# The last batch's group norm moved one step forward into other PSUM banks, and one clearing moved behind the first mixed input, in a two-layer kernel

## The chip, the cores and the metric

The kernel runs on one core of a Trainium2 chip. The metric is the device time of one execution in microseconds (us). The kernel before was run three times: median 1484.47 us, lowest 1482.65, highest 1484.83. One more execution was taken with the hardware profiler; its rows are used below.

## The reference, cut to what matters

16 batches of 112 tokens by 512 channels go through two layers. The first is a cross attention over 375 context rows. The second is an RWKV block, and only this one is touched. For each batch:

```python
xa = ln(x); sx = shift(xa) - xa
xxx = tanh((xa + sx * maa_x) @ maa_w1)          # the "mixed input" xa + sx * maa_x
xk, xw, xv, xr, xg = xa + sx * (maa_stack + xxx @ maa_w2)
w = exp(-exp(time_decay + tanh(xw @ td_w1) @ td_w2))
r, k, v, g = xr @ Wr.T, xk @ Wk.T, xv @ Wv.T, silu(xg @ Wg.T)
# scan over the tokens, state per head: out = r (u k v + s);  s = k v + w s
m, va = mean(out), var(out)                     # per head: the group norm
og = (out - m) / sqrt(va + 1e-5) * gn_w + gn_b
x1 = x + og * g @ Wo.T
xc = ln(x1); xk2, xr2 = xc + sx2 * ffn_maa_k, xc + sx2 * ffn_maa_r
return x1 + sigmoid(xr2 @ Wfr.T) * (square(relu(xk2 @ Wfk.T)) @ Wfv.T)
```

## The kernel before

All five engines run instruction streams written out by hand, ordered by semaphores. The first phase (`cross_attention`) does the first layer for all batches and writes each result to DRAM. Then `rwkv_block`, the second phase, begins with a barrier.

The second phase is a pipeline of 18 steps over 16 batches, three batches deep. `step(n)` does `pre` for batch n (layer norm, mixing, the projections r, k, v, g), `scan` for batch m = n - 1 (the recurrence over chunks of 8 tokens), and `post` for batch l = n - 2 (group norm, output projection, second layer norm, feed-forward part). A batch is one tile: channels on 128 partitions, 4 groups of channels times 112 tokens = 448 elements in the free direction. Each engine has its own `step` function, which writes down the order of these parts on that engine. TensorE's is unrolled over all 18 steps; the other engines loop over pairs of steps.

Steps at the ends are thin. Step 0 has `pre` only. Step 16 has `scan` of batch 15 (the last) and `post` of batch 14. Step 17 has `post` of batch 15 alone.

The PSUM banks are dealt out by role. `pre_bank` (three banks, b_bank3 to b_bank5) serves the layer norm's transposes, the mixing and the projections. `post_bank` (b_bank6 and b_bank7) serves everything in `post`. So batch l's mean (`gn_mean`, L1660, into `post_bank[0]`) waits until the batch before it has read its feed-forward result out of that bank (`s_ff`, incremented by `finish`, L1178).

The chain of the last batch, with its lines: `wkv_sum` on DVE (L1128), `gn_mean` on PE (L1660), `centre` on DVE (L1136), `square` on ACT (L1401), `gn_var` on PE (L1667), `gn_rstd` on ACT (Ln L1407, Exp L1409, each behind a table load), `group_norm` on DVE (L1141), `gn_affine` on ACT (L1268), `gate_output` on POOL (L926), `project_out` on PE (L1504 with b_wo), `residual` and second layer norm on DVE (L1146 to L1155), transposes on PE (L1491), `xc_affine` on ACT, `ffn_input` on DVE (L1167), `ffn_key` (L1498 with b_wfk), `ffn_receptance` (b_wfr) and `ffn_value` (b_wfv) on PE, `finish` on DVE (L1178, L1181) and the store. The centred values live in `cen` and their squares and inverse deviations in `sq`; `cen` is also the input xr2 of `ffn_receptance`.

The start of the second phase, with its lines: statistics of batch 0 on DVE, `rstd1` (L882) and `xa_state` (L887) on POOL, `apply1` on DVE (L1010), transposes on PE, `xa_affine` on ACT, `token_shift` (L1018) and `mix_input` (L1023) on DVE. Behind `mix_input`, DVE runs `setup` (L984 to L990: seven small tensor_scalar operations on constants). PE then does `maa_first` (L1522, L1524) and `maa_second` (L1552); DVE does `mix` (L1034), POOL adds (`mix`, L899), PE goes on with `decay_first` (L1562). On POOL, `zero_blocks` (L873 to L878) stands directly behind `xa_state`: five memsets of the buffers wz, kz, vbd and first. Their values are first needed by ACT's `decay_factor` near the end of step 0.

Of the kernel before, what the change touches and what calls it, by code (L numbers as in the profile page):

```python
# [678 lines left out]
def rwkv_block(nc, A, ident, vec, W, w_loaded, K, k_loaded):  # L679
# [3 lines left out]
    with ExitStack() as ctx:  # L683
# [94 lines left out]

        def by_chunk(flat):

            return flat.rearrange("p (c b s) -> p c b s", c=C, s=CH)
# [82 lines left out]
        def _(pool):  # L864
# [54 lines left out]
            def gate_output(l, scan):  # L919
                pool.wait_ge(s_gaff, count(l, 1, 1))  # L920
                pool.wait_ge(s_g, count(l, 1, 1))
                if at_least(l, 1):
                    pool.wait_ge(s_wo, count(later(l, -1), 1, 1))
                if scan:
                    pool.wait_ge(s_bonus, count(later(l, 1), 1, 1))
                pool.tensor_tensor(gated[:], sq[:], gate2[:, l[1]], ALU.mult).then_inc(s_gated, 1)  # L926
# [54 lines left out]
        def _(dve):  # L981
# [149 lines left out]
            def centre(l):  # L1131
                dve.wait_ge(s_mean, count(l, 1, 1))
                if at_least(l, 1):
                    dve.wait_ge(s_gaff, count(later(l, -1), 1, 1))
                    dve.wait_ge(s_fr, count(later(l, -1), 1, 1))
                dve.tensor_tensor(cen[:].rearrange("p c t -> p (c t)"), wkv[:].rearrange("p c t -> p (c t)"),  # L1136
                                  post_bank[0][:, 0:CT], ALU.subtract).then_inc(s_cen, 1)

            def group_norm(l):
                dve.wait_ge(s_grs, count(l, 1, 1))  # L1140
                dve.tensor_tensor(cen[:], cen[:], sq[:], ALU.mult).then_inc(s_gnorm, 1)  # L1141
# [42 lines left out]
            def step(n, pre, scans, post, first):  # L1184
# [13 lines left out]
                if post:  # L1198
                    wkv_sum(l)
# [17 lines left out]
                if post:  # L1217
                    centre(l)
# [4 lines left out]
                if post:  # L1223
                    group_norm(l)
# [38 lines left out]
        def _(act):  # L1263
# [133 lines left out]
            def square(l):  # L1397
                act.wait_ge(s_cen, count(l, 1, 1))
                if at_least(l, 1):
                    act.wait_ge(s_gated, count(later(l, -1), 1, 1))  # L1400
                act.activation(sq[:], cen[:], ACT.Square).then_inc(s_sq, 1)  # L1401

            def gn_rstd(l):

                act.wait_ge(s_var, count(l, 1, 1))
                flat = sq[:].rearrange("p c t -> p (c t)")
                act.activation(flat, post_bank[1][:, 0:CT], ACT.Ln, bias=ln_eps[:, 0:1]).then_inc(s_ln2, 1)  # L1407
                act.wait_ge(s_ln2, count(l, 1, 1))
                act.activation(flat, flat, ACT.Exp, scale=-0.5).then_inc(s_grs, 1)  # L1409

            def gn_affine(l):
                act.wait_ge(s_gnorm, count(l, 1, 1))
                affine(lambda c: sq[:, c], lambda c: cen[:, c], half_gn[:, 0], half_gn[:, 1]).then_inc(s_gaff, 1)
# [23 lines left out]
            def step(n, pre, scans, post, first):  # L1437
# [18 lines left out]
                if post:  # L1456
                    square(l)
                if pre:
                    decay_rate(n)
                if post:  # L1460
                    gn_rstd(l)
                    gn_affine(l)
# [12 lines left out]
                if post:  # L1475
                    relu_square(l)
                    receptance(l)

# [3 lines left out]
        def _(pe):  # L1482
# [173 lines left out]
            def gn_mean(l):  # L1656
                pe.wait_ge(s_wkv, count(l, 1, 1))
                if at_least(l, 1):
                    pe.wait_ge(s_ff, count(later(l, -1), 1, 1))
                pe.matmul(post_bank[0][:, 0:CT], headmean[:], wkv[:].rearrange("p c t -> p (c t)"), start=True,  # L1660
                          stop=True).then_inc(s_mean, 1)

            def gn_var(l, scans):
                pe.wait_ge(s_sq, count(l, 1, 1))
                if scans:
                    pe.wait_ge(s_bv, count(later(l, 1), 1, 1))
                pe.matmul(post_bank[1][:, 0:CT], headmean[:], sq[:].rearrange("p c t -> p (c t)"), start=True,  # L1667
                          stop=True).then_inc(s_var, 1)

            def project_out(l):  # L1670
                pe.wait_ge(s_gated, count(l, 1, 1))
                token_major(post_bank[0], weight(l, "wo"), gated).then_inc(s_wo, 1)
# [5 lines left out]
            def ffn_key(l):  # L1678
                pe.wait_ge(s_xk2, count(l, 1, 1))
                channel_major(post_bank[0], weight(l, "wfk"), xk2).then_inc(s_fk, 1)  # L1680
# [9 lines left out]
            def step(n, pre, scans, post, first):  # L1690
# [15 lines left out]
                if post:  # L1706
# [6 lines left out]
                if post:  # L1713
                    gn_var(l, scans)
# [121 lines left out]
```

## Time and profile before

| what | value |
|---|---|
| median of 3 runs | 1484.47 us (1482.65 to 1484.83) |
| the profiled execution's own time | 1483.6 us |
| its span (first to last instruction) | 1481.8 us |
| mean granted TensorE clock over the span | 0.973 |
| busy share PE / DVE / ACT / POOL | 94% / 60% / 49% / 33% |
| second phase | from about 653 us to the end |

Times in the trace are counted from the start of the span. "Busy" of an engine leaves out waits. A row of the timeline gives start, duration, engine, line, operation, the tiles written and read, and in square brackets the idle time of the engine before it and who ended it. In the names, `b_bank` stands for any of the eight banks, `xk` for xk2, `rk` is also `gated`, `x` for x2, `ln_tok` also for ln2_tok, which `receptance` writes. One matmul instruction in float32 shows as two MATMUL records (x8 is four instructions).

### The profile page before, as it was taken

What the parts mean: (1) busy time and instruction counts of PE and PEld (TensorE: products, weight loads), DVE (VectorE), ACT (ScalarE), POOL (GpSimd) and SP (SyncE); (2) the same over time, 40 slices, a digit from 0 to 9 for tenths busy, and PEclk for the clock granted to TensorE, in tenths of its full rate; (3) what the DMA queues carried; (4) which work ended last, traced back from release to release, by engine and by line L of the source; (5) the groups of instructions that cost most, each with busy time, mean ns of one, the idle gap of its engine ahead of it and who ended that gap; (6) DMA issues with size and microseconds to landing.
All of it is one profiled execution on the core that took longest, in us unless ns stands there. A gap on an engine that the chain in (4) does not pass through costs nothing. (4 is left out here: it accounts for less than half of the span.)

```text
span 1481.8 us, 41201 instructions
## 1 busy us (share of the span) xinstructions
PE 1388.5 (94%) x16448; PEld 1007.6 (68%) x16448; DVE 888.9 (60%) x2287; ACT 722.5 (49%) x1772; POOL 486.7 (33%) x530
## 2 busy tenths in 40 slices
PE   5999999999999999947989999999999999999965
PEld 4777777777777777626766667666676666666632
DVE  3444444444444443433887788887878878787751
ACT  3666666666666666521245344443444434444422
POOL 2211111111111111011543456434554345543330
PEclk9999999999999999968899999999999999999997
DMA  7531111111111100012001000011000010010000
GB/s 217 152 92 41 41 41 40 39 39 39 39 38 35 34 24 14 7 32 105 11 20 27 27 20 9 25 26 26 19 10 26 26 27 8 20 26 21 20 13 6
DMA packets 25686, 54.97 MB, mean 37 GB/s; under 512 B 3984, under 2 KB 6672, under 8 KB 24016
## 3 DMA queue, kind: packets, MB, share of 16 engines
q1 hardware_dynamic: 25552, 52.99, 12.4%
q8 instruction: 108, 1.77, 0.5%
q14 instruction: 26, 0.21, 0.0%
HBM read 42.23 MB, written 7.34 MB: 33 GB/s over the span
## 5 line engine op out<-in xcount | busy, mean ns | idle before, releaser
L907 POOL TENSOR_TENSOR rst<-rp,st 128x448 f32<-128x448 f32 x192 | 193.9, 1029 | 74.4 <-DVE st L1105 49.7
L270 POOL TENSOR_TENSOR aT_lo<-whole,aT_hi 128x375 fp32r<-128x375 f32 x64 | 58.6, 916 | 443.9 <-ACT whole L422 441.1
L342 DVE CUSTOM_DVE_ANT_0 probs<-a_bank,unmask 112x375 f32<-112x375 f32 x256 | 126.0, 545 | 79.7 <-PE a_bank L539 72.4
L899 POOL TENSOR_TENSOR xm<-mixed,xa 128x448 f32<-128x448 f32 x80 | 87.8, 1097 | 240.6 <-DVE mixed L1034 239.1
L441 ACT ACTIVATE probs<-probs,least 112x375 f32<-112x375 f32 x256 | 153.8, 607 | 0.0
L348 DVE RECIPROCAL inv_rows<-sums 112x128 f32<-112x128 f32 x64 | 61.0, 953 | 153.9 <-ACT probs L441 153.9
L450 ACT COPY probsT<-a_bank 125x448 f32<-125x448 f32 x192 | 90.1, 535 | 51.7 <-PE a_bank L594 51.7
L1034 DVE SCALAR_TENSOR_TENSOR mixed<-b_bank,vec_sb,sx 128x112 f32<-128x112 f32 x320 | 83.1, 328 | 53.5 <-PE b_bank L1552 52.7
L594 PEld LDWEIGHTS a_bank<-ident_sb,probs 112*125 112x125 f32 x768 | 90.8, 188 | 30.9 <-ACT keyT L432 16.3
L594 PE MATMUL a_bank<-ident_sb,probs 112*125 112x112 f32 x768 | 99.3, 279 | 2.7 <-ACT probs L441 2.7
L537 PE MATMUL a_bank<-aT_hi,wk_lo 128*128 128x376 f32 x256 | 91.1, 356 | 1.7 <-issue 1.7
L539 PE MATMUL a_bank<-aT_hi,wk_hi 128*128 128x376 f32 x256 | 85.3, 333 | 0.0
L538 PE MATMUL a_bank<-aT_lo,wk_hi 128*128 128x376 f32 x256 | 84.8, 331 | 0.0
L537 PE MATMUL a_bank<-wv_hi,aT_lo 128*126 128x512 f32 x192 | 79.9, 416 | 0.0
L1268 ACT ACTIVATE xa<-b_bank,vec_sb 128x112 f32<-128x112 f32 x64 | 23.2, 444 | 110.0 <-POOL xm L899 88.9
L538 PE MATMUL a_bank<-wv_lo,aT_hi 128*126 128x512 f32 x192 | 75.7, 394 | 0.0
L539 PE MATMUL a_bank<-wv_hi,aT_hi 128*126 128x512 f32 x192 | 75.6, 394 | 0.0
L1113 DVE TENSOR_TENSOR rst<-rp,st 128x448 f32<-128x448 f32 x64 | 74.9, 1171 | 0.7 <-PE b_bank L1609 0.7
L1084 DVE TENSOR_TENSOR bv<-bv,ktil 128x392 f32<-128x392 f32 (+6 forms) x112 | 69.5, 621 | 3.8
L436 ACT COPY value<-a_bank 125x512 f32<-125x512 f32 x48 | 28.1, 586 | 85.6 <-PE a_bank L539 85.6
L1504 PE MATMUL b_bank<-b_wo,rk 128*112 128x512 f32 x128 | 61.8, 629 | 7.2 <-POOL rk L926 7.2
L1609 PE MATMUL b_bank<-rst,b_collect 128*32 128x448 f32 x512 | 58.3, 548 | 6.3 <-DVE rst L1113 5.3
(167 smaller groups left out, 3100.0 us busy)
## 6 DMA issues: line engine op xcount, KB each, us to landing
ctx_tok<-in_ctx SPq DMA_DIRECT2D x16, 750.0 KB
xT_sb<-in_xT SPq DMA_DIRECT2D x16, 224.0 KB, 9.7
x_tok<-in_x SPq DMA_DIRECT2D x16, 224.0 KB, 9.4
x_between_layers<-x_sb SPq DMA_DIRECT2D x16, 224.0 KB, 2.3
b_x<-x_between_layers SPq DMA_DIRECT2D x16, 224.0 KB, 2.7
x_post<-x_between_layers SPq DMA_DIRECT2D x16, 224.0 KB, 2.8
out_dram<-fin SPq DMA_DIRECT2D x16, 224.0 KB, 2.3
vbd<-vtok SPq DMA_DIRECT2D x208, 16.0 KB
```

What stands on the lines that cost most here:

```text
L342: dve.tensor_tensor_reduce(out=probs[:, g % 2, i], in0=score_bank[i][0:T, 0:TC], in1=unmask[:, m[1]], scale=-SCALE, scalar=-LOWEST, op0=AL ...
L441: act.activation(probs[:, g % 2, i], probs[:, g % 2, i], ACT.Exp, scale=-1.0, bias=least[:, g % 2, i:i + 1], accum_out=sums[:, g % 2, i:i ...
L450: act.copy(probsT[:, g % 2, k], unit_bank(n, f"P{g}{k}")[0:TK, 0:HG * T]).then_inc(s_ringev, 1)
L537: pe.matmul(dst, ll, rh, start=start, stop=False)
L538: pe.matmul(dst, lh, rl, start=False, stop=False)
L539: return pe.matmul(dst, lh, rh, start=False, stop=stop)
L594: last = pe.transpose(dst[0:TK, i * T:(i + 1) * T], probs[:, g % 2, i, k * TK:(k + 1) * TK], ident[0:T, 0:T])
L899: pool.tensor_tensor(xm[:, f % 2], mixed[:, f % 2], xa[:, :, 1:T + 1], ALU.add).then_inc(s_xm, 1)
L907: pool.tensor_tensor(by_chunk(rst[:, j % NPROD]), by_chunk(rp[:].rearrange("p c t -> p (c t)")), state_of(j), ALU.mult).then_inc(s_pprod, 1)
L1034: last = dve.scalar_tensor_tensor(out=mixed[:, f % 2, c], in0=src[:, c * T:(c + 1) * T], scalar=vec[:, VEC[MIXES[f]], c:c + 1], in1=sx[:, ...
L1084: dve.tensor_tensor(dst, dst, vprod[:, :, 0:CH - d], ALU.add).then_inc(s_acc, 1)
L1113: dve.tensor_tensor(by_chunk(rst[:, j % NPROD]), by_chunk(rp[:].rearrange("p c t -> p (c t)")), state_of(j), ALU.mult).then_inc(s_vprod, 1)
```

## The change

It does two things.

1. On POOL, `zero_blocks` waits for the first mixed input of batch 0 (`s_xin`, incremented by the last instruction of `mix_input`) before its first memset.

2. For the last batch alone (`is_last`), `wkv_sum`, `gn_mean`, `centre`, `square`, `gn_var`, `gn_rstd`, `group_norm` and `gn_affine` are issued in step 16 instead of step 17. The mean goes to `pre_bank[0]`, the variance to `pre_bank[1]`, the output projection to `pre_bank[2]`; the centred values and squares live in `xm[:, 0]` and `xm[:, 1]`, since the last batch's projections have read these by then. New waits stand for the new owners of these buffers: `s_mixed`, `s_r`, `s_g`, `s_gmm`, and `s_fin` and `s_ff` of the batch in front where `post_bank[0]` and x2 are used again.

```diff
+        def is_last(l):
+            return is_batch(l, B - 1)
+        def norm_home(l):
+            return (xm[:, 0], xm[:, 1]) if is_last(l) else (cen[:], sq[:])
+        def norm_bank(l):
+            return (pre_bank[0], pre_bank[1]) if is_last(l) else (post_bank[0], post_bank[1])
+        def out_home(l):
+            return pre_bank[2] if is_last(l) else post_bank[0]
...
             def zero_blocks():
+                pool.wait_ge(s_xin, 1)
                 pool.memset(wz[:], 0.0)
...
             def centre(l):
                 dve.wait_ge(s_mean, count(l, 1, 1))
-                if at_least(l, 1):
+                if is_last(l):
+                    dve.wait_ge(s_gmm, count(l, 1, 1))
+                elif at_least(l, 1):
...
             def residual(l):
                 dve.wait_ge(s_wo, count(l, 1, 1))
                 dve.wait_ge(s_x1p[l[1]], 16 * (l[0] + 1))
+                if is_last(l):
+                    dve.wait_ge(s_fin, count(later(l, -1), 1, 1))
-                dve.tensor_tensor(x2[:], post_bank[0][0:T, :], x1p[:], ALU.add).then_inc(s_x2, 1)
+                dve.tensor_tensor(x2[:], out_home(l)[0:T, :], x1p[:], ALU.add).then_inc(s_x2, 1)
...
# VectorE's step (and "if post and not is_last(l)" where these three stood)
                 if post:
                     ffn_input(l, xk2, "ffn_k", s_xk2)
+                    if is_last(m):
+                        wkv_sum(m)
                     ffn_input(l, xr2, "ffn_r", s_xr2)
+                if is_last(m):
+                    centre(m)
+                    group_norm(m)
...
# ScalarE's step
                 if post:
                     relu_square(l)
+                if is_last(m):
+                    square(m)
+                if post:
                     receptance(l)
+                if is_last(m):
+                    gn_rstd(m)
+                    gn_affine(m)
...
             def gn_mean(l):
                 pe.wait_ge(s_wkv, count(l, 1, 1))
-                if at_least(l, 1):
+                if is_last(l):
+                    pe.wait_ge(s_mixed, count(l, MAA, MAA))
+                elif at_least(l, 1):
                     pe.wait_ge(s_ff, count(later(l, -1), 1, 1))
...
# TensorE's step
                 if post:
                     ffn_key(l)
+                if is_last(m):
+                    gn_mean(m)
+                if post:
                     ffn_receptance(l)
+                if is_last(m):
+                    gn_var(m)
```

Nothing is added to or taken from the work; no DMA is moved. The order of instructions is shown at three places, with the line numbers of each kernel's own file (the change shifts them). The first is PE at the end of the program, the kernel before: the last rows of step 16, then step 17 (from the second L1660 on).

```order
L1498 MATMUL b_bank6<-xk2,b_wfk 64x112 x32
L1504 MATMUL b_bank7<-b_wfr,cen 112x512 x4
L1504 MATMUL b_bank6<-b_wfv,xk2 112x512 x4
L1660 MATMUL b_bank6<-wkv,b_headmean 128x448
L1667 MATMUL b_bank7<-sq,b_headmean 128x448
L1504 MATMUL b_bank6<-b_wo,rk 112x512 x4
L1491 MATMUL b_bank7<-ident_sb,ln2_tok 128x112 x4
```

The same stretch of PE in the changed kernel.

```order
L1531 MATMUL b_bank6<-xk2,b_wfk 64x112 x32
L1695 MATMUL b_bank3<-wkv,b_headmean 128x448
L1537 MATMUL b_bank7<-b_wfr,cen 112x512 x4
L1704 MATMUL b_bank4<-xm,b_headmean 128x448
L1537 MATMUL b_bank6<-b_wfv,xk2 112x512 x4
L1537 MATMUL b_bank5<-b_wo,rk 112x512 x4
L1524 MATMUL b_bank7<-ident_sb,ln2_tok 128x112 x4
```

The mean and the variance of batch 15 now stand on either side of batch 14's receptance, ahead of batch 14's ffn_value, in banks 3 and 4.

The second is ACT at the same place, before: relu and square of batch 14's key, its tanh, then batch 15's square, logarithm and exponential.

```order
L1427 ACTIVATE xk2<-b_bank6 128x448
L1429 ACTIVATE xk2<-xk2 128x448
L1435 ACTIVATE ln2_tok<-b_bank7 112x512
L1401 ACTIVATE sq<-cen 128x448
L1407 ACT_TABLE_LOAD
L1407 ACTIVATE sq<-b_bank7,b_eps 128x448
L1409 ACT_TABLE_LOAD
```

And in the changed kernel.

```order
L1454 ACTIVATE xk2<-b_bank6 128x448
L1456 ACTIVATE xk2<-xk2 128x448
L1428 ACTIVATE xm<-xm 128x448
L1462 ACTIVATE ln2_tok<-b_bank7 112x512
L1434 ACT_TABLE_LOAD
L1434 ACTIVATE xm<-b_bank4,b_eps 128x448
L1436 ACT_TABLE_LOAD
```

Batch 15's square moved ahead of batch 14's tanh; the two table loads stand directly behind the tanh.

The third is POOL at the start of the second phase in the changed kernel.

```order
L890 MEMSET wz 128x1080 [waits xin_ready]
L891 MEMSET kz 104x1024
L892 MEMSET vbd 104x4096
L893 MEMSET chunk_first 128x540
L895 MEMSET chunk_first 128x4x14 [waits first_cleared]
```

The order of the rows is that of before (there L873 to L878); only the wait for xin_ready is new.

## Rows read from the trace of the kernel before

**Rows 1.** The page: its first line.

```profile
span 1481.8 us, 41201 instructions
```

**Rows 2.** Windows: stretch, length, busy per engine, granted clock, DMA share, GB/s.

```profile
650.00:698.00 48.00, 25.74 (x396) 23.08 (x396) 18.32 (x48) 6.56 (x22) 13.25 (x18) 0.75 0.27 103
767.03:1325.44 558.41, 556.54 (x8118) 381.46 (x8116) 451.89 (x1046) 243.29 (x565) 270.18 (x276) 1.00 0.08 21
```

**Rows 3.** Timeline of the second phase's start, up to the first transposes.

```profile
657.23 0.19 POOL L887 COPY xa<-b_rows 128x4 f32<-128x4 f32 x1
657.31 6.15 DVE L1010 TENSOR_SCALAR ln_tok<-b_x,ln_mv,ln_rs 112x512 f32<-112x512 f32 x1 [0.78 <-POOL ln_rs L882]
657.36 1.00 POOL L873 MEMSET wz<- 128x1080 f32 x1
...
663.25 0.36 POOL L878 MEMSET chunk_first<- 128x56 f32 x1
```

**Rows 4.** Line L1010 alone: min/median/max ns over its 16 instructions.

```profile
L1010 DVE TENSOR_SCALAR ln_tok<-b_x,ln_mv,ln_rs x16: 535/544/6154, 657.3 to 1325.4; 112x512 f32<-112x512 f32 x16
```

**Rows 5.** Timeline, from the mixed input to the first decay product.

```profile
666.78 1.07 DVE L1023 SCALAR_TENSOR_TENSOR xin<-sx,vec_sb,xa 128x112 f32<-128x112 f32 x4
...
668.04 0.87 DVE L990 TENSOR_SCALAR bonus_w<-b_same_head,vec_sb 128x128 f32<-128x128 f32 x4
...
673.03 1.06 DVE L1034 SCALAR_TENSOR_TENSOR mixed<-b_bank,vec_sb,sx 128x112 f32<-128x112 f32 x4 [4.12 <-PE b_bank L1552]
...
674.15 1.43 PE L1552 MATMUL b_bank<-th,b_maa 32*64 32x112 f32 x16 [1.14 <-DVE mixed L1034]
674.17 1.05 POOL L899 TENSOR_TENSOR xm<-mixed,xa 128x448 f32<-128x448 f32 x1 [10.57 <-DVE mixed L1034]
...
675.50 1.75 PE L1562 MATMUL b_bank<-xm,b_td 128*64 128x112 f32 x8
```

**Rows 6.** Timeline: VectorE beside GpSimd's unbroken run, and GpSimd beside VectorE's.

```profile
720.88 3.75 POOL L907 TENSOR_TENSOR rst<-rp,st 128x448 f32<-128x448 f32 x4
720.95 4.04 DVE L1084 TENSOR_TENSOR bv<-bv,ktil 128x336 f32<-128x336 f32 x1
...
783.92 2.30 POOL L917 TENSOR_TENSOR rk<-rec,key 128x448 f32<-128x448 f32 x1 [2.67 <-ACT rec L1333]
...
784.15 1.06 DVE L1023 SCALAR_TENSOR_TENSOR xin<-sx,vec_sb,xa 128x112 f32<-128x112 f32 x4
```

**Rows 7.** Timeline of the program's end, to the output projection of batch 15.

```profile
1433.75 3.69 PE L1504 MATMUL b_bank<-b_wfr,cen 128*112 128x512 f32 x8
...
1434.45 0.58 ACT L1429 ACTIVATE xk<-xk 128x448 f32<-128x448 f32 x1
...
1437.48 0.60 ACT L1435 ACTIVATE ln_tok<-b_bank 112x512 f32<-112x512 f32 x1 [2.45 <-PE b_bank L1504]
...
1441.74 0.99 PE L1660 MATMUL b_bank<-wkv,b_headmean 128*128 128x448 f32 x2 [0.87 <-DVE fin L1178]
...
1442.77 0.62 DVE L1136 TENSOR_TENSOR cen<-wkv,b_bank 128x448 f32<-128x448 f32 x1 [0.45 <-PE b_bank L1660]
...
1444.02 1.28 ACT L1407 ACT_TABLE_LOAD   x1
...
1451.38 6.06 PE L1504 MATMUL b_bank<-b_wo,rk 128*112 128x512 f32 x8 [6.30 <-POOL rk L926]
```

**Rows 8.** TensorE's timeline, a full step: what follows the mean's matmul.

```profile
895.94 1.02 PE L1660 MATMUL b_bank<-wkv,b_headmean 128*128 128x448 f32 x2
896.89 0.99 PE L1569 MATMUL b_bank<-ttd,b_td 128*64 128x112 f32 x16
```

**Rows 9.** Windows over projections out (batch 14, batch 15) and key (batch 15).

```profile
1414.81:1420.19 5.38, 5.38 (x8) 1.87 (x8) 1.20 (x3) 0.00 (x0) 4.87 (x5) 0.68 0.00 2
1451.38:1457.44 6.06, 6.06 (x8) 2.17 (x8) 0.00 (x0) 0.00 (x0) 0.00 (x0) 0.60 0.00 0
1464.89:1470.57 5.68, 5.68 (x65) 5.54 (x65) 0.93 (x4) 0.00 (x0) 0.00 (x0) 0.56 0.00 0
```

More of the change, by code:

```diff
@@ L1197, in step @@
                         decay_key(m, d)
-                if post:
+                if post and not is_last(l):
                     wkv_sum(l)
@@ L1216, in step @@
                     mix(n, 2)
-                if post:
+                if post and not is_last(l):
                     centre(l)
@@ L1222, in step @@
                     product(m, 3)
-                if post:
+                if post and not is_last(l):
                     group_norm(l)
@@ L1398, in square @@
                 act.wait_ge(s_cen, count(l, 1, 1))
-                if at_least(l, 1):
+                if at_least(l, 1) and not is_last(l):
                     act.wait_ge(s_gated, count(later(l, -1), 1, 1))
-                act.activation(sq[:], cen[:], ACT.Square).then_inc(s_sq, 1)
+                act.activation(norm_home(l)[1], norm_home(l)[0], ACT.Square).then_inc(s_sq, 1)
             def gn_rstd(l):
                 act.wait_ge(s_var, count(l, 1, 1))
-                flat = sq[:].rearrange("p c t -> p (c t)")
-                act.activation(flat, post_bank[1][:, 0:CT], ACT.Ln, bias=ln_eps[:, 0:1]).then_inc(s_ln2, 1)
+                flat = norm_home(l)[1].rearrange("p c t -> p (c t)")
+                act.activation(flat, norm_bank(l)[1][:, 0:CT], ACT.Ln, bias=ln_eps[:, 0:1]).then_inc(s_ln2, 1)
                 act.wait_ge(s_ln2, count(l, 1, 1))
@@ L1455, in step @@
                     tanh_td(n)
-                if post:
+                if post and not is_last(l):
                     square(l)
@@ L1459, in step @@
                     decay_rate(n)
-                if post:
+                if post and not is_last(l):
                     gn_rstd(l)
@@ L1657, in gn_mean, with gn_var @@
                 pe.wait_ge(s_wkv, count(l, 1, 1))
-                if at_least(l, 1):
+                if is_last(l):
+                    pe.wait_ge(s_mixed, count(l, MAA, MAA))
+                elif at_least(l, 1):
                     pe.wait_ge(s_ff, count(later(l, -1), 1, 1))
-                pe.matmul(post_bank[0][:, 0:CT], headmean[:], wkv[:].rearrange("p c t -> p (c t)"), start=True,
+                pe.matmul(norm_bank(l)[0][:, 0:CT], headmean[:], wkv[:].rearrange("p c t -> p (c t)"), start=True,
                           stop=True).then_inc(s_mean, 1)
-            def gn_var(l, scans):
+            def gn_var(l):
                 pe.wait_ge(s_sq, count(l, 1, 1))
-                if scans:
+                if is_last(l):
+                    pe.wait_ge(s_r, count(l, 1, 1))
+                else:
                     pe.wait_ge(s_bv, count(later(l, 1), 1, 1))
-                pe.matmul(post_bank[1][:, 0:CT], headmean[:], sq[:].rearrange("p c t -> p (c t)"), start=True,
+                pe.matmul(norm_bank(l)[1][:, 0:CT], headmean[:], norm_home(l)[1].rearrange("p c t -> p (c t)"), start=True,
                           stop=True).then_inc(s_var, 1)
@@ L1679, in ffn_key @@
                 pe.wait_ge(s_xk2, count(l, 1, 1))
+                if is_last(l):
+                    pe.wait_ge(s_ff, count(later(l, -1), 1, 1))
                 channel_major(post_bank[0], weight(l, "wfk"), xk2).then_inc(s_fk, 1)
@@ L1705, in step @@
                     decay_first(n)
-                if post:
+                if post and not is_last(l):
                     gn_mean(l)
@@ L1712, in step @@
                     attend_near(m, 1)
-                if post:
-                    gn_var(l, scans)
+                if post and not is_last(l):
+                    gn_var(l)
                 if pre:
```

15 lines of the change are left out of this document (9 added, 6 removed).

## The prediction

> **What bounds the kernel now.** I read the page first, for the span of 1481.8 us [rows 1], then the windows over the stages. In the twelve full steps of the second phase TensorE is busy for 556.5 of 558.4 us at full granted clock [rows 2]; the change leaves those steps alone, and nothing it does there could show. What is left are the ends. The first 48 us of the second phase have TensorE busy for 25.7 us, at a mean clock of 0.75 [rows 2], so there a chain through all engines sets the time; the same holds for the end, where one batch is alone. So the next view is the timeline of each end, read link by link: who starts when, and who was waited for.
>
> At the start the striking row is DVE's L1010, the normalisation of batch 0: 6.15 us [rows 3], where the median of its 16 runs is 0.544 [rows 4]. TensorE's first transposes wait for it. It began at 657.31, while POOL ran L887 (657.23 to 657.42), and ended at 663.46. POOL's clearing began at 657.36 and its last memset started at 663.25 [rows 3]. So the normalisation was held as long as POOL had one instruction ready behind the other, and was let go at the first pause. The same thing shows elsewhere: L1084, started 0.07 us behind a run of four products on POOL that ended at 724.63, ended at 724.99 [rows 6].
>
> At the end the chain of batch 15 begins with its mean, at 1441.74, and what it waited for is batch 14's finish on DVE, which frees the bank (the row's bracket names fin). From there the chain goes to the output projection at 1451.38, with TensorE idle for 6.30 us before it [rows 7].
>
> **The change, the start.** Without memsets behind L887, L1010 runs as its median: from 657.31, plus at most the 0.11 us that L887 still lasts, it ends near 657.86 instead of 663.46. That is **5.60 us** off the chain. In what follows I keep the times of before and speak of delays against them.
>
> The clearing itself now starts with the mixed input, whose last instruction ends at 667.85. What is next on each engine? On DVE the setup, seven small tensor_scalars without a pause, the last ending at 668.91 [rows 5]. They are of L1010's kind, so one of the two must wait. DVE is in the middle of its run when POOL wakes, and rows 6 show how that goes the other way round as well: POOL's L917, started at 783.92 while DVE ran without a pause, took 2.30 us and ended at 786.22, 1.01 after the end of DVE's mixed input (785.21), so it did next to nothing before. I take it that the clearing waits for the setup's end. It lasts from 657.36 to 663.61, 6.25 us [rows 3], so it runs from 668.91 to 675.16. Behind it on POOL stands the first add L899, which before began at 674.17 and took 1.05 [rows 5]: now it ends at 676.21. Who waits for it is decay_first (L1562), which began at 675.50, when TensorE was through with L1552 anyway. So 0.7 us are given back, and the chain behind (decay, the projection of v) moves by it. Bounds: 0 if setup and clearing pass each other (the clearing then ends by 674.3), 1.9 and more in the first rival. Net of the start: **-4.9 us**. The cleared buffers are asked for only at the end of step 0, so their being late costs nothing. DVE's own mix L1034, at 673.03, reads PSUM and one SBUF tile; I take it as undisturbed. The Trainium skill (SBUF — State Buffer, "Who interferes with whom") says that a VectorE instruction with at most one SBUF input outside the two-port modes does not contend with GpSimd; no row of this trace shows it beside a memset.
>
> **The change, the end.** Moving wkv_sum between the two inputs of batch 14's feed-forward part delays the second by about 0.6 us (the centring, an operation of the same shape, takes 0.62), hidden under ffn_key on TensorE, behind which the receptance began only at 1433.75 [rows 7]. Now gn_mean is issued there, at 1433.75. Its matmul holds TensorE for 0.95 us (895.94 to 896.89) [rows 8], so batch 14's receptance runs from 1434.70 and ACT's tanh, which ended at 1438.08, ends at 1439.03. The mean is there at 1434.74, the centring (0.62) at 1435.4, the square at 1436.0: ACT is free, since its last square of the key ends at 1435.03, and it waits for the receptance anyway. gn_var follows the receptance at 1438.1 and is through by 1439.2. So the chain now hangs on ACT: the table load of the logarithm follows the tanh, at 1439.04, where it came at 1444.02 [rows 7]; it ends after the variance is there. From that load to the output projection all links are as before (7.36 us). The projection starts **4.98 us** earlier.
>
> What is put back: batch 14's ffn_value ended at 1440.87 (the mean at 1441.74 less its idle 0.87) and now ends at 1442.8, two matmuls of 0.95 later, and its finish on DVE with it. The finish now stands behind group_norm of batch 15, which ends near 1443.5, and ahead of the residual, which waits for a projection that begins at 1446.4: hidden, with some 6 us to spare. The idle time of TensorE before the projection shrinks from 6.30 to 3.6 us. The projection of batch 15 took 6.06 us at a granted clock of 0.60, that of batch 14, with matmuls sparse before it but no long gap, 5.38 at 0.68 [rows 9]. At full clock eight such records take 3.69 (L1504, rows 7); at half clock throughout it would be about 7. I take 5.38, the row of the same instruction with less idle time before it: **0.68 us** more. The bounds are 2.4 gained and 0.9 lost. The key's 5.68 us at a clock of 0.56 [rows 9] can move by as much: half clock throughout would add 0.8, a clock that rises earlier would take off up to 2. I leave it.
>
> **The sum.** Start -4.9, end -4.98 - 0.68: -10.5 us. The profiled execution took 1483.6 us (span 1481.8), 0.9 below the median of the three runs; it becomes 1473.1, and the median of 1484.47 becomes **1474.0**, 0.7% less. A measurement of this kernel can tell about 0.2%, 3 us.
>
> **The rivals.**
>
> *The clearing holds the setup (0.20).* If POOL's memsets get in between two of DVE's small instructions, L990 waits for the run's end as L1010 did. The clearing then runs from 667.9 to 674.2, the setup ends at 674.9 instead of 668.91, the first mix starts at 674.9 instead of 673.03, and the transfer to decay_first is late by 1.9 instead of 0.7: 1475.2. For it speaks that L1010 lost against exactly this run; against it, that L917 had to wait for DVE's run.
>
> *They take turns (0.06).* Each waits for the other's one instruction. L1010 then should have come in after the first memset, at 658.4, and it did not [rows 3]; so little speaks for it. Five setup instructions beside the first four memsets (6.0 us) and about 1.2 us of their own: the setup ends near 675.2, 2.2 us late at the first mix: 1475.5. This is what the Trainium skill's page (SBUF — State Buffer, "SBUF: two separate sides") would give: the pair of ports goes to whoever starts first, for the whole instruction, and the other blocks. By that rule, taken for one instruction at a time, the time would be 1475.5. Rows 3 and 6 show a hold over a whole run of instructions instead.
>
> *The clearing is not what held L1010 (0.06).* Then something else at that moment did, the store or loads of x1 for example, and only the end gains, 5.7 us: 1478.8. Against it: L1010 ends within 0.3 us of the clearing's first pause.
>
> *The end does not gain (0.05).* The waits for other banks or an unlucky order on ACT eat it, for instance when the receptance's input comes late behind wkv_sum and the tanh with it; every microsecond that the tanh ends later than 1439.03 is lost in full. At 5 us it is all gone: 1479.6.
>
> *Slower (0.03).* The one mechanism that could turn the sign is TensorE's clock in the thin steps. The start ran at a mean clock of 0.75 [rows 2], falling and rising with the work, and the change shifts when the work comes. A busy microsecond's work at 2.4 GHz takes two at 1.2, so each further microsecond at the lower level costs up to 0.5. To eat 10.5 us, 21 further microseconds of busy TensorE would have to run at the lower level; from there on the kernel is slower. With 30 it would be 1474.0 + 15 = 1489.0. Against it: the twelve full steps ran at 1.00, the thin steps around them keep their order, and the gaps at both ends get shorter.
>
> **How the numbers follow.** The forecast has 0.60. The range takes in it and the two rivals of the lock: 1475.5 plus 1.7 us for a clock that stays low in the last projections and plus the spread of the runs, 1478.0 at the top; at the bottom 1474.0 less 0.7 (no collision), less 1.7 for a projection at full clock, less 1.3 for the key and the spread: 1470.3. That leaves out the other three rivals and little more. Faster by over 0.2% (below 1481.5) are all cases but the last: 0.95, with 0.03 for no change to be seen, where small losses add up to one of the weak rivals, and 0.02 for slower.
>
> **What would show it.** Start: L1010's counterpart lasts 0.5 to 0.7 us; the memsets start right behind the setup, and the first add on POOL behind them, about 2 us after the mix. If the last of the setup lasts 6 us, it is the first rival; if each is stretched a little, the second. End: the logarithm's table load directly behind batch 14's tanh, and the projection out 7.4 us behind that load. The twelve full steps keep their 46.5 us each (558.4 / 12). The forecast is wrong if L1010 stays long, if the projection starts less than 4 us closer to batch 14's receptance than before, or if the clock in either end differs by more than a tenth.

## The result, and the profile after

The changed kernel took 1474.41 us in the median of 11 runs (1472.26 to 1480.41), the kernel before, in 11 runs beside it, 1484.33 (1482.65 to 1485.79). The ratio is 0.9944 with a 95% interval of 0.993 to 0.9959: faster by 0.4 to 0.7%. Two more comparisons of the same kernel, told below, gave 0.9933 and 0.9952. The forecast was 1474.0 in a range of 1470.3 to 1478.0.

The profiled execution took 1472.61 us. Its page begins:

```profile
span 1470.8 us, 41203 instructions
...
PE 1388.6 (94%) x16448; PEld 1009.8 (69%) x16448; DVE 885.2 (60%) x2287; ACT 723.2 (49%) x1772; POOL 486.3 (33%) x530
```

The span is 11.0 us shorter than before [rows 1]. Of this, 1.1 us lies in the first phase, which the change does not touch: the second phase's first statistics on DVE start at 654.34, before at 655.43. From there to the start of the last instruction on DVE the changed kernel is 9.9 us shorter. All comparisons of profiles below are counted from that first statistics instruction for this reason.

The start of the second phase in the timeline of the changed kernel (its lines are higher than those of before: by 17 on DVE and POOL, by 27 on ACT, by 33 on PE):

```profile
656.15 0.19 POOL L904 COPY xa<-b_rows 128x4 f32<-128x4 f32 x1
656.23 0.55 DVE L1027 TENSOR_SCALAR ln_tok<-b_x,ln_mv,ln_rs 112x512 f32<-112x512 f32 x1 [0.78 <-POOL ln_rs L899]
656.83 1.01 PE L1524 MATMUL b_bank<-ident_sb,ln_tok 112*128 112x112 f32 x4 [8.54 <-DVE ln_tok L1027]
...
660.09 1.07 DVE L1040 SCALAR_TENSOR_TENSOR xin<-sx,vec_sb,xa 128x112 f32<-128x112 f32 x4
...
661.22 1.15 POOL L890 MEMSET wz<- 128x1080 f32 x1 [4.89 <-DVE xin L1040]
...
661.35 2.20 DVE L1007 TENSOR_SCALAR bonus_w<-b_same_head,vec_sb 128x128 f32<-128x128 f32 x4
662.31 1.09 POOL L891 MEMSET kz<- 104x1024 f32 x1
...
663.36 3.65 POOL L892 MEMSET vbd<- 104x4096 f32 x1
...
665.39 1.77 PE L1585 MATMUL b_bank<-th,b_maa 32*64 32x112 f32 x32 [0.69 <-ACT th L1310]
...
667.18 1.06 DVE L1051 SCALAR_TENSOR_TENSOR mixed<-b_bank,vec_sb,sx 128x112 f32<-128x112 f32 x4 [3.63 <-PE b_bank L1585]
667.55 0.20 POOL L895 MEMSET chunk_first<- 128x56 f32 x1
...
668.32 1.05 POOL L916 TENSOR_TENSOR xm<-mixed,xa 128x448 f32<-128x448 f32 x1 [0.58 <-DVE mixed L1051]
```

The normalisation takes 0.55 us in place of 6.15 [rows 3]. The clearing starts in the middle of the setup, not behind it. The setup's four L1007 take 2.20 us (0.87 before, rows 5), and each of the first three memsets 0.14 or 0.15 more than before: they took turns. The setup is over at 663.55, though, and the first mix is not due before 667.18. POOL's first add starts 0.08 us behind the mix. The last memset ends at 667.75, 0.49 us before the mix does. So the collision cost nothing.

The end, TensorE and ACT and what releases them, in the same kernel:

```profile
1429.42 1.02 PE L1695 MATMUL b_bank<-wkv,b_headmean 128*128 128x448 f32 x2
...
1430.28 3.60 PE L1537 MATMUL b_bank<-b_wfr,cen 128*112 128x512 f32 x8
...
1431.13 0.58 ACT L1428 ACTIVATE xm<-xm 128x448 f32<-128x448 f32 x1 [0.44 <-DVE xm L1155]
1433.71 0.92 PE L1704 MATMUL b_bank<-xm,b_headmean 128*128 128x448 f32 x2
1433.91 0.60 ACT L1462 ACTIVATE ln_tok<-b_bank 112x512 f32<-112x512 f32 x1 [2.20 <-PE b_bank L1537]
1434.46 3.60 PE L1537 MATMUL b_bank<-b_wfv,xk 128*112 128x512 f32 x8
1434.53 1.28 ACT L1434 ACT_TABLE_LOAD   x1
...
1441.89 5.20 PE L1537 MATMUL b_bank<-b_wo,rk 128*112 128x512 f32 x8 [3.83 <-POOL rk L943]
...
1454.14 5.45 PE L1531 MATMUL b_bank<-xk,b_wfk 128*64 128x112 f32 x64 [3.31 <-DVE xk L1189]
```

The table load stands directly behind the tanh, and the output projection 7.36 us behind the table load, to the hundredth as before. From the end of the key's products of batch 14 (1433.75 before, 1429.42 now) to the output projection it is 12.47 us in place of 17.63 [rows 7].

The gain by stages, from three profiles of the changed kernel (the first and the two repeats below), each counted from the second phase's first statistics and compared with before:

| stretch | before | changed kernel, three profiles |
|---|---|---|
| to the normalisation of the third batch (start) | 70.14 | 66.48, 66.79, 67.58 |
| from there to the normalisation of the 16th (full steps) | 599.87 | 599.91, 599.09, 598.93 |
| from there to the start of the last instruction on DVE (end) | 152.94 | 146.66, 147.57, 147.24 |

So the start gave 2.6 to 3.7 us, the end 5.4 to 6.3 in these profiles.

### The profile page after: what moved, and what is told of

It reads as the page before. It is cut to its first block and busy times, and to the rows that moved or that the text cites. A ratio compares the mean times of both kernels' runs of the same rounds, so it can differ in the third digit from the quotient of the medians.

```text
span 1470.8 us, 41203 instructions
## 1 busy us (share of the span) xinstructions
PE 1388.6 (94%) x16448; PEld 1009.8 (69%) x16448; DVE 885.2 (60%) x2287; ACT 723.2 (49%) x1772; POOL 486.3 (33%) x530
## 3 DMA queue, kind: packets, MB, share of 16 engines
q8 instruction: 108, 1.77, 0.5%
```

## The experiments

Each kernel was profiled once and then timed in rounds beside the kernel before. In the comparisons the kernel before had 1484.41 us (26 runs, with the first four kernels), 1484.08 (16, the next four) and 1484.86 (17, the last four).

### One part at a time

The clearing alone, on the kernel before:

```diff
             def zero_blocks():
+                pool.wait_ge(s_xin, 1)
                 pool.memset(wz[:], 0.0)
```

> The kernel before, with only the wait for the first mixed input ahead of the clearing. Theory (the start and the end gain separately): about 5 us less than before, L1010 back at 0.55 us, and the end as before, with the output projection of batch 15 7.4 us behind its table load. Rival (the clearing is not what held L1010): no change, L1010 stays at 6 us. Rival (the gain is the end's alone): no change.

Measured: 1481.15 us (1475.78 to 1482.96, 12 runs), ratio 0.997, interval 0.9957 to 0.9983. In the profile L1010's counterpart takes 0.55 us, the start is 66.35 us long (before 70.14), the end 154.07 (before 152.94; 0.7 of the 1.1 us is batch 14's output projection, which took 6.05 us in this profile and 5.38 in that of before [rows 9]). The table load and the output projection of this kernel are those of before, 7.36 us apart:

```profile
1441.23 1.28 ACT L1408 ACT_TABLE_LOAD   x1
...
1448.59 5.76 PE L1505 MATMUL b_bank<-b_wo,rk 128*112 128x512 f32 x8 [6.30 <-POOL rk L927]
```

The end alone:

```diff
             def zero_blocks():
-                pool.wait_ge(s_xin, 1)
                 pool.memset(wz[:], 0.0)
```

> The changed kernel without the wait ahead of the clearing. Theory: 5 to 6 us less than before, L1010 at 6.15 us as before, the output projection of batch 15 5 us closer to batch 14's receptance. Together with the run of the start alone the two differences add up to the whole, 10 to 11 us. Rival (the end gives nothing): as before.

Measured: 1477.14 us (1475.48 to 1483.31, 9 runs), ratio 0.9957, interval 0.994 to 0.9974. L1010's counterpart takes 6.16 us, the end 147.90. The medians of the two parts, -3.26 and -7.27 us, add up to -10.5; the whole had -9.9 in both its first comparisons. The two gains are separate and add up, and the clearing was what held the normalisation. By medians the start gave less than the 4.9 us forecast, the end more than the 5.7; the intervals (2.5 to 6.4 us for the start, 3.9 to 8.9 for the end) hold both forecasts.

### What held the normalisation

The kernel before with pauses in POOL's run, and nothing else:

```diff
-                pool.memset(wz[:], 0.0)
-                pool.memset(kz[:], 0.0)
-                pool.memset(vbd[:], 0.0)
+                pool.memset(wz[:], 0.0).then_inc(s_gap, 1)
+                pool.wait_ge(s_gap, 1)
+                pool.memset(kz[:], 0.0).then_inc(s_gap, 1)
+                pool.wait_ge(s_gap, 2)
+                pool.memset(vbd[:], 0.0).then_inc(s_gap, 1)
+                pool.wait_ge(s_gap, 3)
```

> The kernel before, with the clearing where it was, but each memset waiting on a semaphore that the one ahead of it raises, so that POOL's run has four pauses. Theory (the normalisation is held as long as POOL has an instruction ready and let go at the first pause): it ends behind the first memset, after 1.3 to 1.7 us in place of 6.15, and the kernel is 3.5 to 4.7 us faster. Rival (the hold lasts for all the memsets, pauses or not, or comes from something else): it stays near 6 us and the time is that of before.

Measured: 1480.04 us (1475.97 to 1482.81, 12 runs), ratio 0.9969, interval 0.9956 to 0.9981. Timeline of the place:

```profile
658.65 1.32 DVE L1014 TENSOR_SCALAR ln_tok<-b_x,ln_mv,ln_rs 112x512 f32<-112x512 f32 x1 [0.78 <-POOL ln_rs L886]
658.70 1.00 POOL L874 MEMSET wz<- 128x1080 f32 x1
659.75 1.11 POOL L876 MEMSET kz<- 104x1024 f32 x1
```

The normalisation ends at 659.97, 0.27 us behind the first memset, as it ended 0.27 behind the fourth before (663.46 against 663.19), and the second memset is the one that now waits, 0.16 us. Here a pause of a semaphore's length was enough to let DVE in. With the clearing left where it was, the kernel has the whole gain of the start alone.

The changed kernel with the clearing earlier, beside DVE's shift and mixed input:

```diff
             def zero_blocks():
-                pool.wait_ge(s_xin, 1)
+                pool.wait_ge(s_ln, 1)
                 pool.memset(wz[:], 0.0)
```

> The changed kernel, with the clearing waiting for the end of the first normalisation (ln) in place of the mixed input, so that it lies beside the transposes, the shift and the mixed input on DVE, and is over about when the setup begins. Theory (a memset stands in the way only of DVE's tensor_scalars out of SBUF): the shift (0.62 us) and the mixed input (1.07 us for four) keep their durations, the setup's four L1007 come back from 2.2 us towards 0.9, and the time is that of the changed kernel within 0.5 us, since the clearing cost it nothing. Rival (any DVE instruction with two SBUF inputs is held by a memset): the shift and the mixed input are late by up to 4 us and the kernel is slower than the changed one by as much.

Measured: 1476.58 us (1472.54 to 1479.74, 11 runs), ratio 0.994, interval 0.9922 to 0.9957, the same as the changed kernel's. Timeline:

```profile
660.18 3.51 POOL L892 MEMSET vbd<- 104x4096 f32 x1
660.95 0.63 DVE L1035 TENSOR_TENSOR sx<-xa 128x448 f32<-128x448 f32 x1 [2.65 <-ACT xa L1295]
661.61 1.07 DVE L1040 SCALAR_TENSOR_TENSOR xin<-sx,vec_sb,xa 128x112 f32<-128x112 f32 x4
662.60 1.12 DVE L1001 TENSOR_SCALAR half_gn<-vec_sb 128x4 f32<-128x4 f32 x1
...
663.64 0.71 POOL L893 MEMSET chunk_first<- 128x540 f32 x1
```

The shift and the mixed input, each with two inputs in SBUF, run at their own 0.63 and 1.07 us in the middle of a memset. The tensor_scalar behind them, on four columns, waits for the memset's end at 663.69. That agrees with the Trainium skill (SBUF — State Buffer, "Who interferes with whom"): an operation with two SBUF inputs is in the way of a GpSimd instruction that reads SBUF, not of one that only writes it, while a tensor_scalar can take the shared pair of ports whole. The setup's four L1007 are back at 1.01 us. So it is the kind of DVE instruction that decides whether a memset is in its way, and L1010 is of the kind that loses.

How many instructions the loser waits for is not settled. Here the tensor_scalar lost to one memset and went ahead of the next, though no pause stands between those two in the program; L1010 lost to four in a row.

### What the clock took back at the start

> The changed kernel once more, for its spread: its 11 runs fell at 1472.3 to 1474.4 (6 of them) and at 1477.8 to 1480.4 (5). Theory (the two levels are TensorE's clock, which falls at another moment in the thin steps at the start from run to run): both levels come again, and a profile of a long run shows more time at the lower clock somewhere in the first two or three steps of the second phase, with the full steps at 46.5 us. Rival: the long runs lose their 6 us in the first phase or spread over all steps; then the level has nothing to do with the change.

The changed kernel again: 1474.49 us (1472.14 to 1479.05, 6 runs), ratio 0.9933, interval 0.9913 to 0.9954. With the third set below, 22 runs lie between 1472.1 and 1480.4 without a clean gap, so the two levels of the first 11 are no longer apart. None of the three profiled runs of this kernel took more than 1476 us, so no profile shows where a run near 1480 loses its time.

Two things on record point to the clock. Each run has its mean granted clock: 0.969 to 0.976 in the 13 runs below 1476 us, 0.967 to 0.972 in the 9 above. And the profile of the kernel with the clearing behind the normalisation (1477.13 us), whose code at the end is that of the changed kernel, has an end of 150.00 us, 2.4 to 3.3 more than the three in the table. In it batch 15's output projection took 6.60 us at a granted clock of 0.55, against 5.20 at 0.70 in the changed kernel's first profile, and the key after it 5.94 at 0.54, against 5.45 at 0.59:

```profile
1444.12 6.60 PE L1537 MATMUL b_bank<-b_wo,rk 128*112 128x512 f32 x8 [3.83 <-POOL rk L943]
```

Whether the longest runs lose all their time in this way is not shown.

The profiles do show where the start lost its microseconds. The first is TensorE of the changed kernel, from the mixing on:

```profile
668.30 1.76 PE L1585 MATMUL b_bank<-th,b_maa 32*64 32x112 f32 x16 [1.14 <-DVE mixed L1051]
...
673.60 3.23 PE L1531 MATMUL b_bank<-xm,b_wv 128*64 128x112 f32 x64
...
683.53 4.95 PE L1531 MATMUL b_bank<-xm,b_wr 128*64 128x112 f32 x64
```

The same pieces before:

```profile
679.15 4.32 PE L1498 MATMUL b_bank<-xm,b_wv 128*64 128x112 f32 x64
...
690.17 3.29 PE L1498 MATMUL b_bank<-xm,b_wr 128*64 128x112 f32 x64
```

The two products of the mixing took 1.00 and 1.43 us before, and now take 1.77 and 1.76; the projection v gains those 1.1 back, and the projection r then loses 1.7. The granted clock, read in two stretches of 1 us each, goes with both. Before, at the mixing and at r:

```profile
672.00:673.00 1.00, 0.99 (x32) 1.00 0.97 410
...
691.00:692.00 1.00, 1.00 (x26) 1.00 0.00 0
```

And in the changed kernel at the same two places:

```profile
666.00:667.00 1.00, 1.00 (x27) 0.50 0.97 410
...
685.00:686.00 1.00, 1.00 (x15) 0.50 0.00 0
```

The third column (behind TensorE's busy time and count) is the clock: 1.00 is 2.4 GHz, 0.50 is 1.2. To test it, the gaps of step 0 were filled with matmuls whose result nobody reads (`ident` times `ident` into a bank that nobody holds; 10, 8, 2, 3 and 8 instructions at five places, of which the first two are shown):

```diff
+            def idle_work(times, weights, columns):
+                for _ in range(times):
+                    pe.matmul(near_bank[0][:, 0:columns.shape[-1]], weights, columns, start=True, stop=True)
...
                 if first:
+                    idle_work(10, ident[:], ident[:])
                     transpose_x(n)
+                    idle_work(8, ident[:], ident[:])
                     maa_first(n)
...
```

> The changed kernel with 31 matmuls whose result nobody reads (128 columns) in TensorE's gaps of step 0. Theory (the start gave back about 1.8 of its 5.6 us because the products of the mixing and the projection r now fall on the lower clock): the stretch from the first normalisation to the second one's successor in step 1 gets shorter by 2 to 5 us, the projection r takes 3.3 us in place of 4.95, and the whole is faster by as much. Rival (the clock is not what took it): no gain beyond 0.5 us, with the 1.8 us still missing.

Measured: 1472.36 us (1468.83 to 1473.09, 6 runs), ratio 0.9919, interval 0.9896 to 0.9942. The start is 61.85 us long, 4.6 less than in the changed kernel's first profile. TensorE:

```profile
667.89 0.99 PE L1585 MATMUL b_bank<-th,b_maa 32*64 32x112 f32 x32
...
670.03 0.98 PE L1585 MATMUL b_bank<-th,b_maa 32*64 32x112 f32 x16 [0.28 <-DVE mixed L1051]
...
683.42 3.29 PE L1531 MATMUL b_bank<-xm,b_wr 128*64 128x112 f32 x64
```

All of step 0's products behind the third filling run at the full clock; the two of `maa_first`, behind the second, still took 1.76 and 1.70 us. So what the start lacks was lost to the lower clock. The clearing is not late there either: the first add starts 0.08 us behind the first mix, at the full clock too. But the last memset ended only 0.03 us before that mix (669.95 and 669.98), so there is no slack left.

The expectation that the whole would be faster by as much did not hold. In this profile the full steps took 601.04 us, 1.1 more than in the changed kernel's longest, and the end 148.01, 0.4 to 1.4 more; batch 15's output projection took 6.67 us at a granted clock of 0.55. From the first statistics on, the profile is 2.2 us shorter than the changed kernel's first, and the medians differ by 2 to 4 us, with intervals that overlap.

### Order or banks

The last batch's group norm in its new banks, but issued in step 17 (the `is_last(m)` blocks out of the four steps, the `not is_last(l)` away):

```diff
-                if post and not is_last(l):
+                if post:
                     gn_mean(l)
...
-                if is_last(m):
-                    gn_mean(m)
                 if post:
                     ffn_receptance(l)
-                if is_last(m):
-                    gn_var(m)
```

> The changed kernel with the last batch's group norm in the projections' banks and in xm, but issued in step 17, where it was. Theory (the order brings the gain, the banks only allow it): the mean starts up to 1 us earlier, right behind ffn_value, but the centring still stands behind the finish of batch 14 on DVE, so at most 0.5 us of the end's gain is left and the kernel is 5 to 6 us slower than the changed one, about 4 us faster than before through the start alone. Rival (the shared bank was what held it): most of the gain stays.

Measured: 1480.51 us (1478.8 to 1483.13, 12 runs), ratio 0.9975, interval 0.9966 to 0.9984. Timeline:

```profile
1436.50 0.92 PE L1685 MATMUL b_bank<-wkv,b_headmean 128*128 128x448 f32 x2
1436.71 0.69 DVE L1200 SCALAR_TENSOR_TENSOR fin<-ln_tok,b_bank 112x512 f32<-112x512 f32 x1 [10.53 <-PE b_bank L1527]
...
1438.04 0.61 DVE L1155 TENSOR_TENSOR xm<-wkv,b_bank 128x448 f32<-128x448 f32 x1
```

The mean no longer waits for the finish, but the centring still stands behind both of finish's instructions on DVE. From the receptance's start (1429.55) to the centring it is 8.49 us, before 9.02 [rows 7]. The free bank alone brings 0.5 us up to the centring; the end is 154.05 us long, as long as that of the clearing alone (154.07). The order brings the rest.

The next link in the order, ACT's tanh of batch 14 ahead of the table load, put behind batch 15's group norm, and the variance ahead of the receptance:

```diff
                 if is_last(m):
                     gn_mean(m)
+                    gn_var(m)
                 if post:
                     ffn_receptance(l)
-                if is_last(m):
-                    gn_var(m)
...
                 if is_last(m):
                     square(m)
-                if post:
-                    receptance(l)
                 if is_last(m):
                     gn_rstd(m)
                     gn_affine(m)
+                if post:
+                    receptance(l)
```

> The changed kernel with the variance's matmul ahead of batch 14's receptance on TensorE, and batch 14's tanh behind batch 15's logarithm, exponential and scaling on ACT. Theory (the last batch's chain now hangs on ACT, whose table load stands behind the tanh): the table load comes 2.8 us earlier, behind the square; the output projection of batch 15 starts 2 to 2.8 us earlier and, TensorE having no gap before it, at the full clock (3.7 us in place of 5.2): 3 to 4 us faster than the changed kernel in the profile. Rival (TensorE's order sets it, not ACT's): no change or slower, since the receptance and the value now end up to 1.4 us later.

Measured: 1470.8 us (1469.59 to 1472.35, 5 runs), ratio 0.991, interval 0.9897 to 0.9923. Timeline:

```profile
1432.27 1.02 PE L1695 MATMUL b_bank<-wkv,b_headmean 128*128 128x448 f32 x2
...
1434.58 1.28 ACT L1434 ACT_TABLE_LOAD   x1
1434.61 1.02 PE L1704 MATMUL b_bank<-xm,b_headmean 128*128 128x448 f32 x2 [1.32 <-ACT xm L1428]
1435.47 3.60 PE L1537 MATMUL b_bank<-b_wfr,cen 128*112 128x512 f32 x8
...
1438.90 3.60 PE L1537 MATMUL b_bank<-b_wfv,xk 128*112 128x512 f32 x8
...
1442.34 3.60 PE L1537 MATMUL b_bank<-b_wo,rk 128*112 128x512 f32 x8
```

The table load stands 2.31 us behind the mean's start, where it was 5.11. The output projection starts 10.07 us behind the mean in place of 12.47, and without a gap in front it takes 3.60 us in place of 5.20. The place behind the tanh was the bound, and now TensorE is: the projection follows ffn_value at once, though POOL's gate product that feeds it was over at 1441.89, 0.45 us earlier. The two orders, ACT's and TensorE's, were changed together; what either gives alone was not run.

### The clock at the end

Unread matmuls in TensorE's three gaps of step 17 (`headmean` times `wkv`, 448 columns, 4, 3 and 4 instructions):

```diff
+                if is_last(l):
+                    idle_work(4, headmean[:], wkv[:].rearrange("p c t -> p (c t)"))
                 if post:
                     project_out(l)
+                if is_last(l):
+                    idle_work(3, headmean[:], wkv[:].rearrange("p c t -> p (c t)"))
...
                 if post:
                     transpose_post(l)
+                if is_last(l):
+                    idle_work(4, headmean[:], wkv[:].rearrange("p c t -> p (c t)"))
```

> The changed kernel with 11 matmuls whose result nobody reads (448 columns, into a bank that is free) in TensorE's three gaps at the end: 4 before the output projection of batch 15, 3 behind it, 4 behind the last transposes. Theory (the projection's 5.20 us and the key's 5.45 us are the lower clock after a gap): they take about 3.6 and 3.3 us, and the kernel is 3 to 4 us faster than the changed one. Rival (these durations come from something else, or the added matmuls end later than the gap): no gain, or a loss of up to 1 us for each gap.

Measured: 1470.23 us (1468.76 to 1473.26, 6 runs), ratio 0.9915, interval 0.9892 to 0.9939. Timeline of TensorE:

```profile
1437.89 3.17 PE L1734 MATMUL b_bank<-wkv,b_headmean 128*128 128x448 f32 x8
1441.88 3.69 PE L1537 MATMUL b_bank<-b_wo,rk 128*112 128x512 f32 x8 [0.82 <-POOL rk L943]
...
1452.61 3.29 PE L1531 MATMUL b_bank<-xk,b_wfk 128*64 128x112 f32 x64 [0.29 <-DVE xk L1189]
```

3.69 for 5.20 us and 3.29 for 5.45, at a granted clock of 1.00 for both, where the changed kernel had 0.70 and 0.59: the whole excess of both was the lower clock.

The profile alone flatters this kernel, though. Batch 14's output projection, which stands ahead of all the added matmuls, took 3.69 us in it and 5.38 in the changed kernel. In the profile of the next kernel it takes 5.38 and the two behind the added matmuls still take 3.69 and 3.29, so these two do not hang on it. Over the 14 profiles of this study batch 14's projection took 3.69 to 6.26 us, at granted clocks of 1.00 to 0.58. So a single profile of the end is uncertain by a microsecond or two, and what a variant is worth is read from the medians.

### Together

The clearing behind the normalisation and unread matmuls at both ends:

> The three together: clearing behind the normalisation, and unread matmuls in the gaps of both ends. If the gains add up: 5 to 9 us less than the changed kernel, near 1467 us. Rival: one undoes the other, no better than the better of the two with unread matmuls.

Measured: 1467.58 us (1465.67 to 1471.17, 6 runs), ratio 0.9894, interval 0.987 to 0.9918. The same with the variance first and batch 14's tanh behind (and without the four unread matmuls ahead of the output projection, whose gap is gone):

> Everything that helped together: clearing behind the normalisation, unread matmuls in the gaps of step 0 and of the end, variance ahead of the receptance. Expected: 2 to 3 us less than the three together without the last (1467.6), near 1465 us. Rival: the order and the unread matmuls give the same microseconds twice, no gain.

Measured: 1463.27 us (1462.86 to 1468.55, 4 runs), ratio 0.9858, interval 0.9844 to 0.9872; the profiled run is the longest of the four. This beats both kernels: 21.6 us less than before, of which the change studied here has 9.9.

The changed kernel a third time, for the spread of its runs:

> The changed kernel a third time, for a profile of one of its long runs (1477.8 to 1480.4; so far both profiled runs were short ones). Theory: a long run differs in TensorE's clock at the ends or in the early steps. Rival: it differs in the first phase, which the change does not touch. If it is a short one again, its spread is one more sample.

Measured: 1476.77 us (1474.84 to 1478.69, 5 runs), ratio 0.9952, interval 0.9939 to 0.9965; the profiled run (1475.57) was again a shorter one. Its span exceeds the first profile's by 2.9 us: 2.2 us of first phase and 1.1 us of start, less 0.4 elsewhere.

## Why the prediction was right

**The normalisation, -5.60 us.** Right to the hundredth: it ended at 0.55 us from its start; the runs with the clearing alone and with pauses show the cause.

**The collision of clearing and setup, +0.7.** Wrong, it cost 0. I took from L917 in rows 6 that POOL would wait for DVE's whole run, where a product on POOL stood beside operations of two inputs; here it is memsets beside tensor_scalars. It did not: the first memset began at 661.22, 0.06 us behind the mixed input, and the clearing was over 0.49 us before the first mix ended. Memset and tensor_scalar took turns, the mechanism that I had given 0.06. The price that I gave that rival (2.2 us late at the first mix) did not hold either: I had the setup last until the fourth memset was through, and it was over at 663.55, during the third, 3.6 us before the first mix.

**The clock at the start, taken as unchanged.** This is the term that I had left out: 1.7 us lost in the projection r (the start's gain is still 5.55 us when r begins, and 3.9 when it ends). The start gave 3.7 us in the first profile where I had 4.9; the step that failed is the sentence that the chain behind decay_first moves by the same amount. Durations of matmuls in a thin stretch are not constants that move along with the chain. The two errors of the start, 0.7 us taken off the gain for nothing and 1.9 us of loss not seen, partly cancelled.

**The end, -4.98 for the output projection's start.** It was 5.16 (17.63 less 12.47). The 0.18 are a shorter hold of the receptance (0.86 us instead of the 0.95 of rows 8) and a receptance of 3.60 instead of 3.69.

**The output projection, -0.68.** 5.20 against 6.06 is -0.86. The key's 5.45 against 5.68 and the transposes' 0.60 against 1.01 gave 0.6 more, which I had left at zero. The end of the changed kernel's first profile is 6.3 us shorter, against 5.7 forecast; those of the repeats are 5.4 and 5.7 shorter. These terms add up to 6.7 us; the other 0.4 was lost ahead of the end of batch 14's key. How close the projection's term came is in part luck: the same instruction took 5.15 to 5.20 us in the three profiles of the changed kernel, but 6.60 and 6.67 in two others with the same code at the end.

**The sum.** The mechanisms of the two main terms held and are shown by the separate runs. That the total came within 0.4 us of the forecast is in good part luck: the start gave 1.2 us less than forecast in the first profile and the end 0.6 more, and the runs of the changed kernel spread over 8 us. The profiled execution (1472.61, forecast 1473.1) had 1.1 us from the first phase as well, which the change does not touch.

**The signs.** The projection came 6.0 us closer to batch 14's receptance, where less than 4 would have refuted the forecast. Two signs were not seen: the memsets did not wait for the setup, and the first add came 0.08 us behind the mix and not 2. The granted clock of the start fell from 0.79 to 0.75, and that from the end of batch 14's key to the last instruction rose from 0.77 to 0.87, just the tenth that I had set as the limit.

**The rivals.** That the clearing was not the cause, that the end would not gain, and that the clock would turn the sign are refuted by the separate runs: each part gained alone. The clock did take something back at the start, but 1.7 us and not 10.5. The full steps kept their 600 us within 1 us.

## What to carry to other kernels

A long DVE instruction beside a queue of GpSimd instructions is worth a look in the timeline even when both are short: four memsets in a row cost 5.6 us on the critical path, and moving them behind one semaphore, or pausing between them, gave most of it back (3.3 and 4.4 us in the medians). Where one item of a pipeline is left alone at the end, issue its chain inside the last full step, and order each engine so that nothing of the item in front stands ahead of it; freeing a buffer alone brings little as long as the order holds it. In the thin stretches here TensorE's gaps cost twice, once as idle time and once as a lower clock for what follows; work to fill them, even unread, gave 4 us at the end of this kernel and 2 to 4 at its start, by the medians.

## What the runs showed of the hardware that was not expected

A tensor_scalar of 112x512 lost to four memsets in a row (6.15 us), but one of 128x4 lost only to the memset that was running (1.12 us) and then went ahead of the next, and four of 128x128 took turns with three memsets. The Trainium skill's rule (SBUF — State Buffer, "SBUF: two separate sides"), that the first to start holds the pair for the whole instruction, fits the last two cases and not the first, nor L1084's 4.04 us beside four products [rows 6]. With a semaphore wait between the memsets the first case followed the rule too (1.32 us). What decides between a hold of one instruction and of a whole run was not found.
